# Two token halves of a gated recurrence: own PSUM banks for each, and attention of the last two tiles ended by halves

## What is computed

```python
# attention, for each of the 8 tiles b
Q = elu(x @ Wq.T + bq) + 1;  K = elu(x @ Wk.T + bk) + 1;  V = x @ Wv.T + bv
KV = einsum('bnd,bne->bde', K, V)
Z = einsum('bnd,bd->bn', Q, K.sum(axis=1) + 1e-6)
x1 = layernorm(x + (einsum('bnd,bde->bne', Q, KV) / Z[..., None]) @ Wo.T + bo)
# recurrence over the 8 tiles, c is (512, 128)
for xt in x1:
    f = sigmoid(xt @ wf.T + c @ uf.T + bf)
    i = sigmoid(xt @ wi.T + c @ ui.T + bi)
    g = tanh(xt @ wc.T + c @ uc.T + bc)
    c = f * c + i * g
# output
h = tanh(x1 @ wo.T + c @ uo.T + bo)
out = layernorm(x1 + h)
```

## Time and profile before

| | us |
|---|---|
| median of 3 runs | 103.58 (103.49 to 103.77) |
| the profiled execution | 102.75 |
| its span in the trace | 101.0 |
| busy in the span: PE, DVE, ACT, POOL | 91.6, 80.9, 68.5, 42.1 |

### The profile page before, as it was taken

One profiled execution on the slowest core, in us unless ns is written; L12 is line 12 of the kernel. 1 busy time (PEld: TensorE's weight loads), 2 busy tenths in 40 slices (PEclk: granted clock), 3 DMA queues, 4 the chain that ended last, 5 costly groups with the idle time before them and its releaser, 6 DMA issues.

```text
span 101.0 us, 1930 instructions
## 1 busy us (share of the span) xinstructions
PE 91.6 (91%) x607; PEld 78.8 (78%) x607; DVE 80.9 (80%) x234; ACT 68.5 (68%) x143; POOL 42.1 (42%) x65
## 2 busy tenths in 40 slices
PE   5989999999799999999999999999999999896700
PEld 4859879688488978978888999989899999785300
DVE  3256598979999996898689989996455999999970
ACT  1465767587497694785869445599365949889760
POOL 2004598148358058019306704260500055455870
PEclk9999999999999999999999999999999999999998
DMA  1869999100000000000000000000000000153366
GB/s 37 295 210 295 401 394 368 46 0 3 0 0 0 0 0 0 10 0 0 0 0 0 6 0 0 0 3 3 6 0 0 0 0 0 47 168 104 104 208 208
DMA packets 5413, 7.36 MB, mean 73 GB/s; under 512 B 507, under 2 KB 3228, under 8 KB 5404
## 3 DMA queue, kind: packets, MB, share of 16 engines
q1 hardware_dynamic: 4972, 6.92, 19.4%
q10 hardware_dynamic: 432, 0.33, 1.2%
HBM read 5.15 MB, written 2.10 MB: 72 GB/s over the span
## 4 chain that ended last, share of the span: by engine, by line
PE 57%; DVE 27%; issue 5%; ACT 4%; POOL 3%; DVEq 0%; POOLq 0%; ACTq 0%
PE ps_ctx L433 7%; PE ps_k L410 6%; PE ps_q L424 6%; PE ps_ctx L453 5%; DVE stats L1140 5%; PE ps_f L397 4%; DVE x L1129 3%; DVE x L960 3%; PE ps_x L467 2%; DVE s L1011 2%; DVE x L975 2%; DVE x L1156 2%; DVE new L1004 2%; PE ps_ctx L443 2%; PE ps_f L481 2%
## 5 line engine op out<-in xcount | busy, mean ns | idle before, releaser
L346 POOL TENSOR_TENSOR s_lo<-s,s_hi 128x512 fp32r<-128x512 f32 (+1 forms) x8 | 8.1, 1012 | 24.6 <-ACT s_hi L752 24.6
L333 POOL TENSOR_TENSOR rstd<-var_eps,minus_half 128x4 f32<-128x4 f32 (+1 forms) x9 | 9.1, 1010 | 12.6 <-DVE var_eps L1148 12.6
L317 POOL TENSOR_TENSOR rstd<-var_eps,minus_half 128x4 f32<-128x4 f32 x8 | 8.6, 1078 | 6.6 <-DVE var_eps L951 6.5
L308 POOL TENSOR_TENSOR k_pair<-k_rows 128x256 f32<-128x256 f32 x8 | 6.3, 782 | 9.1 <-DVE k_rows L986 9.1
L960 DVE TENSOR_SCALAR x<-x,stats,rstd 128x128 f32<-128x128 f32 x26 | 10.0, 441 | 0.0
L805 ACT ACTIVATE x_hi<-ps_x 128x512 fp32r<-128x512 f32 x8 | 4.8, 594 | 6.2 <-PE ps_x L467 6.2
L736 ACT ACTIVATE th_f<-ps_f,half_b 128x256 f32<-128x256 f32 (+1 forms) x11 | 5.8, 530 | 4.4 <-PE ps_f L513 4.3
L410 PE MATMUL ps_k<-wkq,x_cols 128*128 128x128 f32 x64 | 8.5, 276 | 0.0
L722 ACT ACTIVATE k_exp<-ps_k,minus_one 128x512 f32<-128x512 f32 x8 | 5.5, 686 | 4.4 <-PE ps_k L418 3.5
L424 PE MATMUL ps_q<-x_cols,wkq 128*128 128x512 f32 x16 | 8.2, 593 | 0.0
L410 PEld LDWEIGHTS ps_k<-wkq,x_cols 128*128 128x128 f32 x64 | 8.0, 194 | 0.2
(11 more groups left out here) (191 smaller groups left out, 286.6 us busy)
## 6 DMA issues: line engine op xcount, KB each, us to landing
x_cols<-xt SPq DMA_DIRECT2D x8, 256.0 KB, 7.0
x_rows<-x SPq DMA_DIRECT2D x8, 256.0 KB, 7.0
out<-x SPq DMA_DIRECT2D x7, 256.0 KB, 2.2
wgate<-w_gate SPq DMA_DIRECT2D x1, 384.0 KB, 6.6
out<-x SPq DMA_DIRECT2D x2, 128.0 KB, 2.0
wkq<-w_kq ACTq DMA_DIRECT2D x1, 131.0 KB, 3.3
wvo_in<-w_vo_in ACTq DMA_DIRECT2D x1, 128.0 KB, 3.3
wout<-w_out SPq DMA_DIRECT2D x1, 128.0 KB, 6.7
```

Of the source, the lines that this page charges most:

```text
L308: nc.gpsimd.tensor_tensor(k_pair[:], k_rows[:, a % 2, 0:C // 2], k_rows[:, a % 2, C // 2:C], ALU.add).then_inc(k_pair_ok, 1)
L317: nc.gpsimd.tensor_tensor(rstd[:, b], var_eps[:, b], minus_half[:], ALU.pow).then_inc(rstd_ok, 1)
L333: nc.gpsimd.tensor_tensor(part_of(rstd, u, T), part_of(var_eps, u, T), minus_half[:, 0:nt * H].rearrange("p (t c) -> p t c", c=H), ALU.pow ...
L346: nc.gpsimd.tensor_tensor(s_lo[:, t % 2, part], state(t)[:, part], s_hi[:, t % 2, part].bitcast(F32), ALU.subtract).then_inc(slo_ok[k], 1)
```

## The change

The gates of second halves get three banks of their own (the two of ps_ctx, and ps_k), columns of the second half; they wait for the last residuals of tiles 6 and 7 that read these banks. The units' banks move accordingly. Tiles 6 and 7 go through residual, statistics, root, normalisation, transposes and the three copies by halves (HALVES: 6 first, 7 first, 6 second, 7 second); DVE normalises the first halves, ACT the second ones. The low part of x1 is made on DVE for first halves, from the copy in SBUF for tiles 6 and 7, and on POOL for the second halves of tiles 5, 6 and 7. The lists of PE, ACT, DVE and POOL are put in a new order: first halves of tiles 6 and 7 are finished before their second halves are begun. The low part of state 9 moves from DVE to POOL. On ACT `normalise(0)` moves from behind the tanhs of step 11 to ahead of them, `out_tanh(2)` from ahead of them to behind; on PE `out_x(2)` and `add_g(2)` move behind the gates of step 11. POOL leaves out the shift of units 7 and 8, which DVE normalises alone.

```diff
@@ -56,7 +56,12 @@
 IN_PSUM = (6, 7, 8)
 
 
-SHARED_LN = (0, 6, 7)
+WHOLE = 6
+HALVES = [(6, 0), (7, 0), (6, H), (7, H)]
+
+
+SHARED_LN = (0,)
+ACT_HALVES = (2, 3)
 
 
 BIAS_BY_PE = 4
@@ -162,9 +167,10 @@
 
         ctx_view = ps_ctx[:, :, 0:2 * DZ].rearrange("p b (c d) -> p b c d", d=DZ)
 
-        g_bank = [ps_x1[:, 0:H * D], ps_i[:, 0:H * D]]
-        unit_bank = [ps_ctx[:, 0, :], ps_ctx[:, 1, :], ps_k[:], ps_q[:], ps_x1[:], ps_ctx[:, 0, :], ps_k[:], ps_q[:],
-                     ps_ctx[:, 1, :]]
+        g_bank = [ps_i[:, 0:H * D], ps_i[:, 0:H * D]]
+        unit_bank = [ps_q[:], ps_c[:], ps_f[:], ps_x1[:], ps_q[:], ps_c[:], ps_f[:], ps_ctx[:, 0, H * D:],
+                     ps_ctx[:, 1, H * D:]]
+        gate_bank = [[ps_f, ps_i, ps_c], [ps_ctx[:, 0], ps_ctx[:, 1], ps_k]]
 
 
         kq_in, vo_in, gate_in, out_in = sem("kq_in"), sem("vo_in"), sem("gate_in"), sem("out_in")
...
@@ -327,8 +350,31 @@
                 pool.wait_ge(bk_in, 16)
                 nc.gpsimd.tensor_scalar(bk_wide[:], bk_wide[:], 1.0, None, ALU.add).then_inc(bk_ok, 1)
 
+            def half_root(j):
+
+                b, c0 = HALVES[j]
+                pool.wait_ge(var_half_ok, j + 1)
+                nc.gpsimd.tensor_tensor(rstd[:, b, c0:c0 + H], var_eps[:, b, c0:c0 + H], minus_half[:, 0:H],
+                                        ALU.pow).then_inc(rstd_half_ok, 1)
+
...
+                                        ALU.mult).then_inc(shift_half_ok, 1)
+
+            def x1_low(b):
+
+                if b < WHOLE:
+                    pool.wait_ge(x1c_ok, b + 1)
+                else:
+                    pool.wait_ge(x1c_half_ok, HALVES.index((b, H)) + 1)
+                nc.gpsimd.tensor_tensor(x1_lo[:, b, H * D:], x1_cols[:, b, H:C].rearrange("p c d -> p (c d)"),
+                                        x1_hi[:, b, H * D:].bitcast(F32), ALU.subtract).then_inc(x1lo_pool_ok, 1)
+
             def second_root(u):
-                pool.wait_ge(var_ok, T + u + 1)
+                pool.wait_ge(var_ok, WHOLE + u + 1)
                 nt = UNITS[u][1]
                 nc.gpsimd.tensor_tensor(part_of(rstd, u, T), part_of(var_eps, u, T),
...
@@ -377,16 +423,23 @@
             reciprocal_root(5)
             key_sums(7)
             state_low(4)
-            reciprocal_root(6)
-            first_shift(6)
+            half_root(0)
+            x1_low(5)
+            half_root(1)
             state_low(5)
-            reciprocal_root(7)
-            first_shift(7)
+            state_low(6)
             state_low(7)
-            state_low(6)
+            half_root(2)
+            half_shift(2)
+            half_root(3)
+            half_shift(3)
+            x1_low(6)
+            state_low(9)
+            x1_low(7)
             for u in range(len(UNITS)):
                 second_root(u)
-                second_shift(u)
+                if DVE_NORM[u] < len(blocks(u)):
+                    second_shift(u)
 
         @block.tensor
         def _(pe):
@@ -467,26 +520,54 @@
                     mm = nc.tensor.transpose(ps_x1[:, c * D:(c + 1) * D], x1[:, b, c], ident[:])
                 mm.then_inc(x1t_mm, 1)
 
-            gates = [(ps_f, f_ok, f_mm), (ps_i, i_ok, i_mm), (ps_c, c_ok, c_mm)]
+            def x1_half_turned(j):
+                b, c0 = HALVES[j]
+                if j == 0:
+                    pe.wait_ge(x1c_ok, WHOLE)
+                else:
+                    pe.wait_ge(x1c_half_ok, j)
+                for i in range(H):
+                    if j in ACT_HALVES:
+                        pe.wait_ge(x1_half_act_ok, ACT_HALVES.index(j) * H + i + 1)
+                    else:
+                        pe.wait_ge(x1_half_ok, j * H + i + 1)
+                    mm = nc.tensor.transpose(ps_x1[:, (c0 + i) * D:(c0 + i + 1) * D], x1[:, b, c0 + i], ident[:])
+                mm.then_inc(x1t_half_mm, 1)
+
+            gates = [(f_ok, f_mm), (i_ok, i_mm), (c_ok, c_mm)]
 
             def gate_x_high(g, k):
 
-                ps, used, _ = gates[g]
+                ps, used = gate_bank[second_half(k)][g], gates[g][0]
                 t, part = STEPS[k][0], columns(k)
                 if k == 0:
                     pe.wait_ge(split_lo, 1)
-                if k >= 1:
-                    pe.wait_ge(used, k)
-                pe.wait_ge(x1hi_ok, t + 1)
+                elif before_in_bank(k) is not None:
+                    pe.wait_ge(used, before_in_bank(k) + 1)
+                elif g == 0:
+                    pe.wait_ge(y_ok, T - 1)
+                elif g == 1:
+                    pe.wait_ge(y_small_ok, T - 1)
+                else:
+                    pe.wait_ge(y_ok, T)
+                if t < WHOLE:
+                    pe.wait_ge(x1hi_ok, t + 1)
+                else:
+                    pe.wait_ge(x1hi_half_ok, HALVES.index(STEPS[k][:2]) + 1)
                 nc.tensor.matmul(ps[:, part], wgate_hi[:, g], x1_hi[:, t, part], start=True, stop=False,
                                  skip_group_check=True)
...
             def gate_x_low(g, k):
-                ps, _, done = gates[g]
+                ps, done = gate_bank[second_half(k)][g], gates[g][1]
                 t, part = STEPS[k][0], columns(k)
-                pe.wait_ge(x1lo_ok, t + 1)
+                if t >= WHOLE - 1 and STEPS[k][1] == H:
+                    pe.wait_ge(x1lo_pool_ok, t - WHOLE + 2)
+                elif t >= WHOLE:
+                    pe.wait_ge(x1lo_half_ok, t - WHOLE + 1)
+                else:
+                    pe.wait_ge(x1lo_ok, t + 1)
                 mm = nc.tensor.matmul(ps[:, part], wgate_hi[:, g], x1_lo[:, t, part], start=False, stop=(t == 0),
                                       skip_group_check=True)
...
@@ -675,26 +757,28 @@
             gates_x(5)
             gates_s(5)
             gates_x(6)
+            x1_half_turned(0)
             gates_s(6)
-            x1_turned(6)
+            gates_x(7)
+            x1_half_turned(1)
+            gates_s(7)
             out_x(0)
-            gates_x(7)
-            gates_s(7)
-            x1_turned(7)
-            out_x(1)
             gates_x(8)
             gates_s(8)
             gates_x(9)
             gates_s(9)
+            x1_half_turned(2)
             out_s(0)
             out_g(0)
             gates_x(10)
             gates_s(10)
+            x1_half_turned(3)
+            out_x(1)
             add_g(1)
+            gates_x(11)
+            gates_s(11)
             out_x(2)
             add_g(2)
-            gates_x(11)
-            gates_s(11)
             out_x(3)
             add_g(3)
             out_x(4)
...
@@ -787,6 +867,25 @@
                 for c in range(H, C):
                     nc.scalar.activation(x1[:, b, c], x1[:, b, c], ACT.Identity, bias=shift[:, b, c:c + 1],
                                          scale=rstd[:, b, c:c + 1]).then_inc(x1_act_ok, 1)
+
+            def half_normalise(j):
+
+                b, c0 = HALVES[j]
+                act.wait_ge(shift_half_ok, ACT_HALVES.index(j) + 1)
+                for c in range(c0, c0 + H):
+                    nc.scalar.activation(x1[:, b, c], x1[:, b, c], ACT.Identity, bias=shift[:, b, c:c + 1],
+                                         scale=rstd[:, b, c:c + 1]).then_inc(x1_half_act_ok, 1)
+
+            def x1_half_high(j):
+                act.wait_ge(x1t_half_mm, j + 1)
+                nc.scalar.activation(x1_hi[:, HALVES[j][0], half_cols(j)], ps_x1[:, half_cols(j)],
+                                     ACT.Copy).then_inc(x1hi_half_ok, 1)
+
+            def x1_half_whole(j):
+
+                b, c0 = HALVES[j]
+                nc.scalar.activation(x1_cols[:, b, c0:c0 + H].rearrange("p c d -> p (c d)"), ps_x1[:, half_cols(j)],
+                                     ACT.Copy).then_inc(x1c_half_ok, 1)
 
             def key_bias(a):
 
@@ -859,30 +958,34 @@
             state_high(4)
             x1_whole(5)
             gates_tanh(5)
-            first_normalise(6)
+            x1_half_high(0)
             state_high(5)
-            x1_high(6)
+            x1_half_whole(0)
             gates_tanh(6)
-            x1_whole(6)
-            first_normalise(7)
+            x1_half_high(1)
+            x1_half_whole(1)
             gates_tanh(7)
-            x1_high(7)
+            state_high(6)
             state_high(7)
-            state_high(6)
             gates_tanh(8)
-            x1_whole(7)
+            half_normalise(2)
             gates_tanh(9)
+            x1_half_high(2)
+            out_tanh(0)
+            x1_half_whole(2)
+            g_high()
             state_high(9)
-            out_tanh(0)
-            g_high()
+            half_normalise(3)
             gates_tanh(10)
+            x1_half_high(3)
+            x1_half_whole(3)
             out_tanh(1)
             state_high(10)
+            normalise(0)
+            gates_tanh(11)
             out_tanh(2)
-            gates_tanh(11)
-            normalise(0)
+            normalise(1)
             out_tanh(3)
-            normalise(1)
             preload(5)
```

(67 more changed lines are left out.)

59 lines of the change are left out of this document (36 added, 23 removed).

## The result

The changed kernel takes 106.06 us in the median of 4 runs (105.42 to 106.34), the kernel before 103.53 (103.34 to 103.77, 4 runs): ratio 1.0234, 95% interval 1.0179 to 1.029. It is 2.5 us slower; the forecast was 1.9 us slower and a time of 105.5.

The account below looks back on a forecast made before the run. No engine is full; a chain of waits through step 11 bounds the kernel, with DVE the bound in the tail. Order +1.3, tail -0.3, waits +0.9 give +1.9 us: 105.5 us, own range 105.0 to 106.0, whole range 104.0 to 106.9.

Parts of the forecast that it names:

- Banks: Gate matmuls of steps 6 and 7: waits for tanhs on the same bank vanish, residual waits replace them; credited nothing.
- Attention by halves: Tiles 6 and 7 by halves: first tanh of step 8 at 71.4 instead of 73.13, 1.7 us gained.
- the two unseen meetings: half_low(0) against state_low(5), state 7 against state_low(6): DVE with two SBUF inputs; taken as nothing, 1.0 kept for the range.
- Step 10 gives some back: Queues on ACT and POOL delay step 10: first tanh 78.2 against 79.29, gain left 1.1 us.
- Step 11 gives back the rest and more: normalise(0) ahead of step 11's tanhs, out_tanh(2) behind: last state ends at 88.1, 1.3 us later than before.
- Tail: After the last state: same order, POOL's shift of unit 7 dropped, 0.3 us saved.
- Waits between DVE and POOL: Operations between SBUF tiles wait for the other engine's, ahead of state 5 and at state 10: +0.9 us.
- The meetings of the shown kind: Variance inside state_low(4) 0.3, half_normalise(0) inside x1_low(5) 0.2, x1_low(7) against state 10 0.4: sum +0.9 us.
- rival A: The two unseen DVE and POOL pairs wait too: +2.9 us, 106.5 us; chance 0.25.
- Rival B: No DVE and POOL pair meets: +1.0 us, 104.6 us; chance 0.20.
- C: PE runs steps 7 to 10 without a gap, POOL's low parts not met: faster, 102.5 us; chance 0.08.
- Rival D: Late step 11 falls in a hole of DVE, no change; chance 0.07, including any result within 0.3% of before.

Follow-up runs that it names:

- banks alone: Kernel before the change with only the new gate and unit banks, their waits, and out_x(1) behind step 10 on PE: 103.73 us, ratio 1.0033.
- State 7 first: Changed kernel with state_high and state_low of step 7 put ahead of those of step 6, as before the change: 105.47 us, ratio 1.0167.
- No meetings: The four orders, plus POOL's x1_low(6) and x1_low(7) waiting until states 9 and 10 are written, and DVE's step 11 right behind residual 2: 103.13 us.
- the four orders: Changed kernel; unit 2 ahead of step 11 (PE, ACT), normalise(0) behind its tanhs, state 7's parts before state 6's, step 10 fed sooner: 103.58 us.
- the low part from PSUM: Changed kernel with DVE's half_low reading the half tile from its PSUM bank instead of the SBUF copy, ACT copying after it: 107.84 us, ratio 1.0438.

## Why the prediction was right

**What bounds the kernel, and where the loss would lie.** Right. The part behind the last state is 14.15 us in the changed kernel against 14.22, and 14.15 to 14.33 in eight of the eleven others. It grows where DVE's work was moved behind that state (16.4 and 14.8), and in "banks alone" (14.5), where I did not trace why; the sum of both stretches stays there (41.59 against 41.53). The whole loss is in the stretch ahead. The signs came out too: counted from state 4 as in the trace before, the first tanh of step 8 is at 72.4 (71.4 to 72.5 were named), that of step 10 at 79.2 (78.2 to 79.5), the end of the last state at 89.2 (88 to 90).

**Banks: nothing.** Right (banks alone: no gain). In the changed kernel step 6 does not wait for the residuals, as forecast. In "banks alone", with whole tiles, it waits 0.55: its first tanh is 0.4 later than in the kernel before (7.40 against 6.99 after state 4), of which 0.1 is left at step 8.

**Attention by halves gains 1.7 us at step 8.** The mechanism is right, the size was not. The first tanh of step 8 is at 12.95 us after the start of state 4 (73.45), before it was at 13.66 (73.13): 0.7 gained. The forecast was 1.7, less the 0.5 that it booked as meetings ahead of state 5. Of the missing 0.5 the two unseen meetings are 0.7 (0.35 and 0.35), less 0.36 that the early ones cost less than thought: the variance of half 0 took 0.31, 0.14 over its 0.17, and half_normalise(0) lost nothing. The remaining 0.15 is not traced.

**Step 10 gives some back.** Right in its place: ACT's queue, then POOL's, 78.33 and 79.02 in the changed kernel, first tanh at 19.73 against 19.82, so 0.1 of the gain was left. Counted were 1.1 less 0.5. What the step gives back was sized rightly, 0.6 in both (1.7 to 1.1, and 0.7 to 0.1); the gain that came to it was too small.

**Step 11 gives back the rest and more.** Third tanh 25.82 after state 4 against 24.70, last state 29.75 against 27.31. From the first tanh of step 10 to the third of step 11 it took 6.09 (forecast 5.99, and 0.4 for the meeting of x1_low(7), which took 1.03 instead of 0.73; 0.3 less than counted), from there to the end of the last state 3.93 (forecast 3.9). The split of it was wrong: I ascribed 1.25 to normalise(0), and taking it away alone gives 0.3, since PE's out_x(2) behind the gates is a second queue in the same place. Putting unit 2 back gives 1.6.

**Tail -0.3.** This step failed. DVE is 0.3 earlier, the end of the span is not (14.15 against 14.22), and with the shift put back it is 14.15 again. I had followed the last operation and not the stores behind it, which hide the saving.

**Waits between DVE and POOL: +0.9.** The size was nearly right by luck, out of two errors. The meetings of the shown kind cost about 0.4 to 0.5 (0.14 and 0.30), not 0.9; the two of the unseen kind, which I took at nothing, cost 0.7. That was the step to take differently. The row that I leaned on, q_cols with its usual 0.68, began 0.1 us ahead of POOL's root, so it could say nothing of a DVE operation that begins second. "State 7 first" shows the price of one of the two: its write falls from 0.77 to 0.42 and the stretch by 0.4. That of half_low(0) is read from the chain and was not taken away alone. "No meetings" shows the same fall for two other writes (1.00 and 0.76 to 0.42), which were slow with the four orders and not in the changed kernel.

The Trainium skill (SBUF — State Buffer, section "Who interferes with whom") had it: a VectorE instruction with two SBUF inputs and a GpSimd instruction that reads SBUF exclude each other. For POOL's low parts the rows agree in both directions (POOL's x1_low(7) stretched to 1.03, DVE's writes to 0.77 and 1.00). For POOL's root they do not agree in the direction that matters here: a keep with two SBUF inputs that began at 67.50 in the kernel before, inside a root from 66.99 to 68.00, took its usual 0.41. The same section says that a VectorE instruction with at most one SBUF input does not wait, outside the two-port performance modes. Statistics (0.43) and the low part from PSUM (0.42) agree. The variance has one SBUF input too and does wait (0.57 and 0.31 instead of 0.17); whether it ran in such a mode no run here shows.

**The sum.** +1.9 forecast, +2.4 in the stretches, +2.5 in the medians. Of the 2.44 us lost ahead of the last state the four meetings are 1.15 (0.14, 0.30, 0.36 and 0.35), which leaves 1.3 for the order of the work: in sum the 1.3 forecast, though not step by step. The rest of the difference is 0.25 more for the meetings (1.15 instead of 0.9) and 0.23 that the tail did not give (0.07 instead of 0.3). The time, 106.06, lies just outside the forecast's own 105.0 to 106.0 and inside the whole range, which was drawn to take in rival A. Rival A (+2.9) had the mechanism of the unseen pairs right and was too dear, since it kept the dear early meetings too; the truth lies between the forecast and A. Rival B and C did not happen: POOL's low parts are met, and PE idles at steps 8 and 10. Rival D neither.

## What to carry to other kernels

When an order is changed on one engine, look for the same unit of work in the queues of the others: the first queue priced hides the next, and only an experiment that moves the unit on all engines shows what it is worth. Mark every operation that reads two tiles in SBUF on DVE, and let no low part of POOL begin just ahead of one that lies on the chain. Whether that pays is read at the next engine: holding POOL back brought two writes from 1.00 and 0.76 to 0.42 us and the tanhs behind them 0.02 us forward, because PE was full in between. A saving behind the last store but one is to be priced at the store, not at the engine.
